# Half of one shared-expert group computed after the last routed group instead of inside the recurrence

## The chip, the cores and the metric

The kernel runs on one core of a Trainium2 chip. The metric is device time in microseconds (us) of one execution. The kernel before takes 687.25 us, the median of three runs (686.86 to 687.51).

## The reference

The input x holds 64 sequences (batch) of 64 steps with 256 features. Two layers follow each other.

1. A recurrent cell (UGRNN) scanned over the 64 steps. Each step needs the state of the step before it:

```
m = concat(x_t, h) @ weight + bias
c = tanh(m[256:]);  g = sigmoid(m[:256] + 1)
h = g * h + (1 - g) * c
```

Its outputs are added to x, which gives x1.

2. A mixture of four experts over x1 with a gate for each sequence, from means of x1 over time. Each sequence uses its best two experts. Expert 1 leaves out steps 21 to 41, expert 2 leaves out steps 0 to 20. One more expert, the shared one, serves every sequence and step. An expert is `gelu(x1 @ w1 + b1) @ w2 + b2` with 1024 hidden features. The output is x1 plus the weighted routed experts plus the shared expert.

## The kernel before, in words

All data lies with the 256 features on the partitions, as K = 2 halves of 128, and (step, sequence) along the free dimension. `acc` holds x, then x1, then the output. `x_hl` holds x1 split into a rounded high part and a low part, since every product is made of three matmuls in fp32r (high by high, low by high, high by low). All work of TensorE is recorded on one line, L722 (`mm`), so its rows are told apart by their tiles: `zy` and `hp` are PSUM.

**Expert groups.** An expert is applied to a group of up to 512 columns. A shared group is 8 steps of 64 sequences (NG = 8 groups, GT = 8 steps). A group passes through 8 chunks (NCH) of 128 hidden features. For a chunk TensorE does layer 1 (6 matmuls into `hp`, L747 to L758) and, two chunks behind, layer 2 (6 matmuls into the `zy` banks, L760 to L772). Between them ScalarE applies gelu (L322) and makes the high part (L327), and VectorE or GpSimd makes the low part (L406 in `split_lo`, or L283). Buffers for chunks are double, so chunk c waits for chunk c-2 at each stage.

**Recurrence.** Step s: 48 small bf16 matmuls of 64 columns for the state (`h_part`, L736, in three parts as the three bf16 parts of the state arrive), tanh on ScalarE (L313), then seven VectorE operations (`cell` L427 and `split_state` L417), four of them on the way to the next state. On the steps whose turn it is, TensorE also computes a quarter of the input part for the four steps to come (`x_part`, L724, 7 matmuls of 256 columns). From the second block of 8 steps on, each step carries as filler one chunk of the shared group whose steps are done (L803 to L815). So shared group 6 is worked on in the last block of 8 steps (`steps(NG - 1, ...)`, L822), and its last four steps have no `x_part`. Then shared group 7 runs alone, with the gate's small matmuls between its chunks (L826 to L847). The gate's arithmetic on VectorE is L509 to L577; between `gate_slots` and the gathering of the first routed group VectorE also writes out shared group 6 (`shared_out`, L603).

**Routed groups.** The gate puts sequences into groups of one expert: 8 sequences of 64 steps (512 columns) or 10 sequences of 44 or 43 steps (440 or 430 columns). The loops over q (the experts in the order 0, 3, 1, 2) and r (their groups) have run-time bounds `sv`. GpSimd gathers the columns of the next group (L285). After each group VectorE weighs its output (`weigh`, L611) and adds it into `acc` for each sequence (`add_slots`, L630), two or three sequences after each chunk of the next group. Sequence numbers are first loaded into registers (L592, L633, L653). `turnover` (L855) interleaves the last two layer-2 chunks of one group with the first two layer-1 chunks of the next.

**Weights.** The queue of the SyncE engine (SP) reads each expert's weights in 8 pieces of 256 KB into a ring of three stage buffers (L217 to L227). ScalarE makes a piece's high part (L333) and VectorE its low part (L414). There are two weight buffers, `w_buf[i % 2]`.

**End.** The last routed group's output is weighed and then added half by half (`add_last`, L656). The output of steps 0 to 20 is written by one DMA once no routed group can change it (L228 and L229), the rest in two DMAs of 1376 KB, one for each half of the features (L232).

Of the kernel before, what the change touches and what calls it, by code (L numbers as in the profile page):

```python
# [13 lines left out]
P = 128  # L14
# [20 lines left out]

ORDER = [E, 0, 3, 1, 2]

# [4 lines left out]
MASKED_EXPERT, MASKED_STEP = 1, HEAD  # L42
PER = [SLOTS if TOKS[e] == T else WIDE for e in ORDER[1:]]
NFULL = sum(p == SLOTS for p in PER)
# [20 lines left out]
def cond_resid_kernel(nc, x, cond, w0, b0, w_exp, small, consts, out):  # L65
    ctx = ExitStack()
    with ctx:
# [45 lines left out]
        con = sb("con", [P, C_END])  # L113
        turn = sb("turn", [P, 2])
        gs = sb("gs", [P, 96])
# [60 lines left out]
        gather_done, yw_done, add_done = sem("gather_done"), sem("yw_done"), sem("add_done")  # L176
        head_ready, out_ready = sem("head_ready"), sem("out_ready")

# [31 lines left out]
        @block.sync  # L210
        def _(sp):
            sp.dma_start(raw_w0[:, 0:K], w0[:, 0:K * 2 * D].rearrange("p (k n) -> p k n", k=K)).then_inc(s_w0, 16)
            sp.dma_start(acc[:, :, 0:GT], x[:, :, 0:GT]).then_inc(s_x0, 16)
            sp.dma_start(con[:], consts).then_inc(s_par, 16)
            sp.dma_start(par[:], small).then_inc(s_par, 16)
            sp.dma_start(acc[:, :, GT:T // 2], x[:, :, GT:T // 2]).then_inc(s_x1, 16)
            for n in range(len(ORDER) * NP):  # L217
                if n == 2:

                    sp.wait_ge(wx_split, K)  # L220
                    sp.wait_ge(wh_split, K)
# [11 lines left out]
            sp.wait_ge(s_out, 16 * (1 + K))  # L233

        @block.gpsimd
        def _(pool):
# [64 lines left out]
            for q in range(E):  # L301
                with pool.Fori(sv[q], sv[q + 1]) as r:
# [3 lines left out]
                    else:  # L306
                        gather(r, q)

        @block.scalar
        def _(act):  # L310
# [51 lines left out]
            with act.Fori(2, NG) as g:  # L362
                for i in range(GT):
                    tanh(g * GT + i, i, i // QT)
                    gelu_chunk(g - 1, i, E, 512)
            for j in range(NCH):
                if j == 1:
# [4 lines left out]
            for q in range(E):  # L372
                e = ORDER[q + 1]
                n = PER[q] * TOKS[e]
                with act.Fori(sv[q], sv[q + 1]) as r:
# [13 lines left out]
                    else:  # L389
                        for j in range(NCH):  # L390
                            gelu_chunk(r + NG, j, e, n)

        @block.vector
        def _(dve):
# [48 lines left out]

            def shared_out(g, y):

                dve.wait_ge(l2_done, (g + 1) * NCH)
                dve.wait_ge(x1_done, (g + 1) * GT)
                for k in range(K):
                    a = acc[:, k, bass.ds(g * GT, GT), :].rearrange("p t b -> p (t b)")
                    last = dve.scalar_tensor_tensor(out=a, in0=y[k], scalar=par[:, S_B2 + E * K + k:S_B2 + E * K + k + 1],  # L450
                                                    in1=a, op0=ALU.add, op1=ALU.add)
                last.then_inc(y_read, 1)
# [49 lines left out]
            with dve.Fori(2, NG) as g:  # L502
                for i in range(GT):
                    if i == 2:
                        shared_out(g - 2, yp)
                    cell(g * GT + i, i)
                    split_lo(g - 1, i, 512)

            def gate_means():  # L509
# [92 lines left out]
            gate_slots()  # L602
            shared_out(NG - 2, yp)  # L603
            dve.wait_ge(list_mm, 1)
# [36 lines left out]

            def slots_at(q, per, i):

                cuts = [0, 3, 6, 8, per] if q == E - 1 and per == WIDE else [min(2 * c, per) for c in range(NCH)]
                return list(range(cuts[i], cuts[i + 1])) if i + 1 < len(cuts) else []

# [3 lines left out]

            def batches(r, a, n):

                return nc.values_load_multi_w_load_instructions(  # L653
                    slot_b[0:1, bass.ds((r + 1) * WIDE + a, n)], engines=(mybir.EngineType.DVE,), min_val=0, max_val=B - 1)[1]

            def add_last(r, e, bs):  # L656

                n = TOKS[e]
                dve.wait_ge(y_read, r + NG + 1)
                for k in range(K):  # L660
                    for s in range(WIDE):
                        dve.wait_ge(add_done, (r + 1 + k) * WIDE + s + 1)
                        dst = tokens_of(acc[:, k:k + 1], e, bs[s])
                        src = y_w[:, k:k + 1, s * n:(s + 1) * n].rearrange("p k (a n) -> p k a n", a=RUNS[e][1])
                        dve.tensor_tensor(dst, dst, src, ALU.add).then_inc(add_done, 1)  # L665
                    dve.wait_ge(add_done, (r + 2 + k) * WIDE + 1)
                    dve.sem_inc(out_ready, 1)

# [9 lines left out]
            for q in range(E):  # L678
                e = ORDER[q + 1]
                n = PER[q] * TOKS[e]  # L680
                with dve.Fori(sv[q], sv[q + 1]) as r:

                    common = NCH - 2 if q == E - 1 else NCH
                    with dve.If(sv[q] < r):
                        for j in range(2, common):
                            split_lo(r + NG, j, n)
                            if slots_at(q, PER[q], j - 2):
                                add_slots(r, q, slots_at(q, PER[q], j - 2))
                    with dve.Else():
                        for j in range(2, common):  # L690
                            split_lo(r + NG, j, n)
                            if q == E - 1 and slots_at(q, PER[q - 1], j - 2):
                                add_prior(r, q, slots_at(q, PER[q - 1], j - 2))
                            elif q and j > 2 and slots_at(q, PER[q - 1], j - 3):
                                add_prior(r, q, slots_at(q, PER[q - 1], j - 3))
# [6 lines left out]
                    bs = []  # L702
                    for j in range(common, NCH):
                        split_lo(r + NG, j, n)
                        bs += batches(r, len(bs), WIDE - 2 if bs else 2)
                    with dve.If(r + 1 < sv[q + 1]):
# [3 lines left out]
                    with dve.Else():  # L710
                        nn = PER[q + 1] * TOKS[ORDER[q + 2]] if q < E - 1 else 0
                        if nn:
                            split_lo(r + NG + 1, 0, nn)
                        weigh(r, q)
                        if nn:
                            split_lo(r + NG + 1, 1, nn)
                        else:
                            add_last(r, e, bs)
        @block.tensor
        def _(pe):  # L720
# [53 lines left out]
            def group_src(g):  # L774
                return lambda part, k: x_hl[:, part, k, bass.ds(g * GT, GT), :]

            y0 = yp

# [12 lines left out]
            def steps(g, filler, carry, last_group=False):  # L791

                for i in range(GT):
                    s = g * GT + i
# [8 lines left out]
                    if filler:  # L803
                        f = g - 1
                        if i == 0:
                            pe.wait_ge(x1_done, g * GT)
                        layer1(f, i, w_of(0), group_src(f), 512, not carry and i < 2)
                        if i == 2 and not carry:
# [3 lines left out]
                        if i >= 2:  # L812
                            layer2(f, i - 2, w_of(0), y0, 512)
                        elif carry:
# [11 lines left out]
            for j in range(NCH):  # L826
# [27 lines left out]

            def turnover(r, i, n, w, y, r2, n2, w2):  # L855

                if n2:
                    pe.wait_ge(piece_done, i * NP + NP // 2)
                    pe.wait_ge(gather_done, r2 + 2)
                for j in range(2):  # L860
                    if n2:
                        layer1(r2 + NG, j, w2, src_of(r2, n2), n2)
                    layer2(r + NG, NCH - 2 + j, w, y, n)
# [74 lines left out]
```

## Time and profile before

| what | value |
|---|---|
| median of three runs | 687.25 us |
| profiled execution, its own time | 687.1 us |
| its span in the trace | 685.3 us |
| TensorE busy | 643.7 us (94%) |
| VectorE busy | 425.8 us (62%) |
| ScalarE busy | 289.8 us (42%) |
| GpSimd busy | 265.4 us (39%) |
| granted TensorE clock, mean | 0.988 |

Times in rows are us from the start of the span. PE is TensorE, DVE is VectorE, ACT is ScalarE, POOL is GpSimd; SPq and DVEq are the sequencers of SyncE and VectorE. In a timeline row the columns are start, duration (to the end of the last instruction merged into the row), engine, line, operation, output tile <- input tiles, count, and in brackets the engine's idle time before it with its releaser. What the chain of waits names is the work that nothing else covered.

### The profile page before, as it was taken

How to read it: one execution, taken by the hardware profiler on the slowest of the kernel's cores; microseconds unless marked ns; L12 is line 12 of the kernel's file. 1: busy time of each engine (PE TensorE's matmuls, PEld its weight loads, DVE VectorE, ACT ScalarE, POOL GpSimd, SP SyncE). 2: the span in 40 equal slices, each digit the busy share in tenths (PEclk: the TensorE clock that was granted, in tenths of full speed). 3: DMA queues.
4: the chain of work that ended last, by engine and by line, in shares of the span. 5: the costliest groups of instructions: out<-in, count | busy, mean ns of one | idle time of the engine just before them, and what ended most of it. 6: DMA issues, size and time to landing. Idle time of an engine off the chain costs nothing.

```text
span 685.3 us, 16932 instructions
## 1 busy us (share of the span) xinstructions
PE 643.7 (94%) x5752; PEld 557.7 (81%) x5752; DVE 425.8 (62%) x942; ACT 289.8 (42%) x485; POOL 265.4 (39%) x531
## 2 busy tenths in 40 slices
PE   2779999999999999999999999999999999999990
PEld 2668888888888888888768888888888999999980
DVE  5798766665656656567766655555547875555453
ACT  3224433333333333333536544544446755544540
POOL 3576646454454554534344433113321343333000
PEclk9999999999999999999999999999999999999995
DMA  6521110000000000000002100000002300000014
GB/s 247 186 64 63 48 32 2 1 0 0 0 0 0 0 0 0 0 2 2 1 0 77 46 0 0 0 0 0 0 0 78 107 18 0 0 0 0 0 64 183
DMA packets 8037, 20.97 MB, mean 31 GB/s; under 512 B 960, under 2 KB 1216, under 8 KB 7488
## 3 DMA queue, kind: packets, MB, share of 16 engines
q1 hardware_dynamic: 7568, 19.64, 8.3%
q10 hardware_dynamic: 432, 0.85, 0.3%
q8 instruction: 21, 0.34, 0.2%
q14 instruction: 16, 0.13, 0.1%
HBM read 16.30 MB, written 4.19 MB: 30 GB/s over the span
## 4 chain that ended last, share of the span: by engine, by line
PE 87%; DVE 6%; DVEq 2%; issue 2%; DMA 1%; ACT 1%; SPq 0%; POOL 0%; ACTq 0%
PE zy L722 53%; PE hp L722 33%; DMA par<-in_small 1%; DVE h_r L421 1%; DVE acc L665 1%; DVEq L633 1%; DVEq L653 1%; DVE d_t L433 1%; DVEq L592 1%; ACT uc L313 1%; DVE shared_buf L595 1%; DVE h_b L423 0%; DVE d_t L431 0%; DVE h_b L436 0%; DVE acc L639 0%
## 5 line engine op out<-in xcount | busy, mean ns | idle before, releaser
L406 DVE TENSOR_TENSOR g_lo<-g_f,g_hi 128x512 fp32r<-128x512 f32 (+2 forms) x176 | 132.9, 755 | 127.7 <-ACT g_hi L327 121.2
L322 ACT ACTIVATE g_f<-hp,par 128x512 f32<-128x512 f32 (+2 forms) x184 | 123.4, 670 | 176.5 <-PE hp L722 174.5
L722 PE MATMUL zy<-g_hi,w_buf 128*128 128x512 f32 (+2 forms) x736 | 190.7, 381 | 0.0
L722 PE MATMUL hp<-shared_buf,w_buf 128*128 (+1 forms) x720 | 173.6, 376 | 1.3 <-DVE shared_buf L595 1.3
L327 ACT ACTIVATE g_hi<-g_f 128x512 fp32r<-128x512 f32 (+2 forms) x184 | 112.9, 613 | 123.5 <-PE zy L722 123.3
L722 PEld LDWEIGHTS zy<-g_hi,w_buf 128*128 128x128 f32 x736 | 138.2, 188 | 22.7
L722 PEld LDWEIGHTS hp<-shared_buf,w_buf 128*128 128x128 f32 x720 | 135.0, 188 | 20.8 <-issue 1.9
L722 PEld LDWEIGHTS zy<-h_b,y_all 128*128 128x128 bf16 x3072 | 94.1, 98 | 27.2 <-issue 15.1
L722 PE MATMUL zy<-h_b,y_all 128*128 128x64 bf16 x3072 | 103.3, 193 | 9.4 <-DVE h_b L436 6.1
L722 PE MATMUL zy<-g_lo,w_buf 128*128 128x512 f32 (+2 forms) x368 | 110.3, 381 | 0.0
L722 PE MATMUL hp<-x_hl,w_buf 128*128 (+1 forms) x384 | 99.8, 395 | 0.3 <-POOL x_hl L254 0.3
L639 DVE TENSOR_TENSOR acc<-acc,y_all 128x128 f32 (+1 forms) x124 | 50.1, 404 | 55.2 <-issue 46.5
L251 POOL TENSOR_TENSOR x_hl<-acc,h_f 128x128 f32 (+1 forms) x64 | 31.8, 497 | 130.1 <-DVE h_f L440 130.1
L296 POOL CAST shared_buf<-x_hl x126 | 79.7, 681 | 0.0
L722 PEld LDWEIGHTS zy<-g_lo,w_buf 128*128 128x128 f32 x368 | 68.9, 188 | 11.8 <-DVE g_lo L406 0.5
L722 PEld LDWEIGHTS hp<-x_hl,w_buf 128*128 128x128 f32 x384 | 68.2, 189 | 12.6 <-POOL x_hl L254 0.8
L292 POOL TENSOR_TENSOR turn<-turn 128x1 f32<-128x1 f32 x14 | 3.4, 246 | 191.9 <-PE hp L722 187.0
L722 PE MATMUL zy<-x_hl,shared_buf 128*128 (+1 forms) x384 | 58.1, 289 | 0.0
L313 ACT ACTIVATE uc<-zy 128x256 f32<-128x256 f32 x64 | 24.6, 385 | 68.9 <-PE zy L722 68.9
L722 PEld LDWEIGHTS zy<-x_hl,shared_buf 128*128 128x128 f32 x384 | 52.3, 197 | 0.0
L241 POOL TENSOR_TENSOR x_hl<-acc,x_hl (+1 forms) x60 | 31.5, 525 | 9.6 <-POOL x_hl L239 8.7
L722 PE MATMUL zy<-shared_buf 128*128 128x256 f32 x64 | 23.5, 368 | 12.1 <-DVE x_hl L482 12.1
(109 smaller groups left out, 433.7 us busy)
## 6 DMA issues: line engine op xcount, KB each, us to landing
stage<-in_w_exp SPq DMA_DIRECT2D x40, 256.0 KB, 2.8
out_y<-acc SPq DMA_DIRECT2D x2, 1376.0 KB, 5.0
acc<-in_x SPq DMA_DIRECT2D x1, 2048.0 KB, 9.1
acc<-in_x SPq DMA_DIRECT2D x1, 1536.0 KB, 9.8
out_y<-acc SPq DMA_DIRECT2D x1, 1344.0 KB, 5.1
acc<-in_w SPq DMA_DIRECT2D x1, 512.0 KB, 4.2
acc<-in_x SPq DMA_DIRECT2D x1, 512.0 KB, 7.2
acc<-in_w ACTq DMA_DIRECT2D x1, 512.0 KB, 5.0
```

The costliest lines, as they stand in the source:

```text
L241: pool.tensor_tensor(x_hl[:, 1, :, bass.ds(s, 1), :], acc[:, :, bass.ds(s, 1), :], x_hl[:, 0, :, bass.ds(s, 1), :].bitcast(F32), ALU.subtr ...
L251: pool.tensor_tensor(hi, a, h_f[:, 1 - i % 2], ALU.add).then_inc(x1_hi, 1)
L296: last = pool.tensor_copy(dst, tokens_of(x_hl, e, bs[s]))
L313: act.activation(uc[:], zb[:, buf, :, :, i % QT, :], ACT.Tanh).then_inc(tanh_done, 1)
L322: act.activation(g_f[:, j % 2, 0:n], hp[j % 2][:, 0:n], ACT.Gelu_apprx_tanh, bias=par[:, S_B1 + e * NCH + j:S_B1 + e * NCH + j + 1]).then_ ...
L327: act.activation(g_hi[:, j % 2, 0:n], g_f[:, j % 2, 0:n], ACT.Copy).then_inc(ghi_done, 1)
L406: dve.tensor_tensor(g_lo[:, j % 2, 0:n], g_f[:, j % 2, 0:n], g_hi[:, j % 2, 0:n].bitcast(F32), ALU.subtract).then_inc(glo_done, 1)
L421: dve.tensor_tensor(h_r[:], h, h_b[:, 0], ALU.subtract).then_inc(hr_done, 1)
L433: dve.scalar_tensor_tensor(out=d_t[:], in0=uc[:, 0], scalar=1.0, in1=d_t[:], op0=ALU.add, op1=ALU.mult).then_inc(q_done, 1)
L592: bs = nc.values_load_multi_w_load_instructions(slot_b[0:1, WIDE:WIDE + SLOTS], engines=(mybir.EngineType.DVE,), min_val=0, max_val=B - 1)[1]
L639: dve.tensor_tensor(dst, dst, y_w[:, :, s * n:(s + 1) * n].rearrange("p k (a n) -> p k a n", a=RUNS[e][1]), ALU.add).then_inc(add_done, 1 ...
L722: return pe.matmul(out_, lhsT=lhsT, rhs=rhs, start=start, stop=stop, skip_group_check=True)
```

## The change

The order of experts becomes `[E, 0, 3, 1, 2, E]`. Of shared group 6 (HELD = 6) only the first four steps (HALF = 256 columns) are computed in the last block of the recurrence and at the start of group 7. The other four steps (52 to 55) are computed after the last routed group, as one more group of 256 columns. For it the shared weights are read again, as pieces 40 to 47. GpSimd makes both their high and low parts, into the buffer that the second last expert leaves. In SP's queue the DMA of output steps 0 to 20 now stands ahead of piece 45, so pieces 45 to 47 are issued behind its wait on `head_ready`. `head_ready` itself is given after all six chunks of the last expert's first group, where two sequences are added after each chunk, and no longer after four of them. The last routed group is added by `add_routed` between the chunks of the final half group, with ten sequence numbers that VectorE loads once after the loop of the first expert. Then steps 21 to 51 and 56 to 63 are written, and last the four held steps.

```diff
-ORDER = [E, 0, 3, 1, 2]
+ORDER = [E, 0, 3, 1, 2, E]
+HELD = NG - 2
+HALF = QT * B
...
@@ sync
+                if n == (len(ORDER) - 1) * NP + NP // 2 + 1:
+                    sp.wait_ge(head_ready, 1)
+                    sp.dma_start(out[:, :, 0:HEAD], acc[:, :, 0:HEAD]).then_inc(s_out, 16)
                 if n >= RING:
                     sp.wait_ge(piece_done, n - RING + 1)
...
-            sp.wait_ge(head_ready, 1)
-            sp.dma_start(out[:, :, 0:HEAD], acc[:, :, 0:HEAD]).then_inc(s_out, 16)
+            held = HELD * GT + QT
+            sp.wait_ge(routed_ready, 1)
+            sp.dma_start(out[:, :, HEAD:held], acc[:, :, HEAD:held]).then_inc(s_out, 16)
+            sp.dma_start(out[:, :, held + QT:T], acc[:, :, held + QT:T]).then_inc(s_out, 16)
             for k in range(K):
                 sp.wait_ge(out_ready, k + 1)
-                sp.dma_start(out[:, k, HEAD:T], acc[:, k, HEAD:T]).then_inc(s_out, 16)
+                sp.dma_start(out[:, k, held:held + QT], acc[:, k, held:held + QT]).then_inc(s_out, 16)
@@ gpsimd, after the gathers
+            pool.wait_ge(l2_done, (sv[E - 1] + NG) * NCH)
+            pool.tensor_tensor(turn[:, 2:3], turn[:, 0:1], turn[:, 0:1], ALU.mult)
+            for m in range(NP):
+                n, c = (E + 1) * NP + m, m * PIECE
+                w = w_of(E + 1)
+                pool.wait_ge(piece_in[n % RING], 16 * (n // RING + 1))
+                pool.tensor_copy(w[:, 0, c:c + PIECE], stage[:, n % RING]).then_inc(piece_hi, 1)
+                pool.wait_ge(piece_hi, n + 1)
+                pool.tensor_tensor(w[:, 1, c:c + PIECE], stage[:, n % RING], w[:, 0, c:c + PIECE].bitcast(F32),
+                                   ALU.subtract).then_inc(piece_done, 1)
@@ vector
-            shared_out(NG - 2, yp)
+            shared_out(HELD, yp, QT)
...
                         if q == E - 1:
-                            dve.wait_ge(add_done, (r + 1) * WIDE + 1)
+                            dve.wait_ge(add_done, r * WIDE + WIDE + 1)
                             dve.sem_inc(head_ready, 1)
...
+                if q == 0:
+                    last_bs = nc.values_load_multi_w_load_instructions(
+                        slot_b[0:1, bass.ds(sv[E] * WIDE, WIDE)], engines=(mybir.EngineType.DVE,), min_val=0, max_val=B - 1)[1]
+            final = sv[E] + NG
+            for j in range(2, NCH):
+                split_lo(final, j, HALF)
+                add_routed(slots_at(PER[E - 1], j - 2), last_bs)
+            dve.wait_ge(add_done, sv[E] * WIDE + WIDE + 1)
+            dve.sem_inc(routed_ready, 1)
+            dve.wait_ge(l2_done, final * NCH + NCH)
+            y = y_bank(sv[E])
+            for k in range(K):
+                a = acc[:, k, HELD * GT + QT:HELD * GT + 2 * QT, :].rearrange("p t b -> p (t b)")
+                dve.scalar_tensor_tensor(out=a, in0=y[k][:, 0:HALF], ..., in1=a, op0=ALU.add, op1=ALU.add).then_inc(out_ready, 1)
@@ tensor
             def steps(g, filler, carry, last_group=False):
+                src, n = (half_src(0), HALF) if last_group else (group_src(g - 1), 512)
...
-                    layer2(f - 1, NCH - 2 + j, w_of(0), y0, 512)
+                    layer2(f - 1, NCH - 2 + j, w_of(0), y0, HALF)
...
-                            turnover(r, 0, n, w, y, r + 1, 0, None)
+                            turnover(r, q + 2, n, w, y, r + 1, HALF, w_of(q + 2), half_src(1))
+            final, w = sv[E] + NG, w_of(E + 1)
+            y = y_bank(sv[E])
+            for j in range(2, NCH):
+                layer1(final, j, w, half_src(1), HALF)
+                if j == 2:
+                    pe.wait_ge(y_read, final - 1)
+                if j % 2 == 0:
+                    pe.wait_ge(piece_done, (E + 1) * NP + NP // 2 + j // 2)
+                layer2(final, j - 2, w, y, HALF)
+            pe.wait_ge(piece_done, (E + 2) * NP)
+            for j in range(NCH - 2, NCH):
+                layer2(final, j, w, y, HALF)
```

ScalarE's gelu of the last block and of the final group follows the same widths (not shown).

## Rows read from the trace of the kernel before

**Rows 1.** The page: granted clock of TensorE in tenths, 40 slices.

```profile
PEclk9999999999999999999999999999999999999995
```

**Rows 2.** The page: the chain that ended last, by engine and line.

```profile
PE zy L722 53%; PE hp L722 33%; DMA par<-in_small 1%; DVE h_r L421 1%; DVE acc L665 1%; DVEq L633 1%; DVEq L653 1%; DVE d_t L433 1%; DVEq L592 1%; ACT uc L313 1%; DVE shared_buf L595 1%; DVE h_b L423 0%; DVE d_t L431 0%; DVE h_b L436 0%; DVE acc L639 0%
```

**Rows 3.** Timeline, the recurrence's last steps and the start of shared group 7.

```profile
306.35 1.57 PE L722 MATMUL zy<-h_b,y_all 128*128 128x64 bf16 x48
...
311.42 1.57 PE L722 MATMUL zy<-h_b,y_all 128*128 128x64 bf16 x48
...
315.68 1.57 PE L722 MATMUL zy<-h_b,y_all 128*128 128x64 bf16 x48
...
325.81 0.39 ACT L313 ACTIVATE uc<-zy 128x256 f32<-128x256 f32 x1 [0.73 <-PE zy L722]
...
328.97 1.67 PE L722 MATMUL hp<-x_hl,w_buf 128*128 128x512 f32 x6 [0.34 <-POOL x_hl L254]
```

**Rows 4.** Timeline, tanh of two steps of the first block, which has no filler.

```profile
35.38 0.38 ACT L313 ACTIVATE uc<-zy 128x256 f32<-128x256 f32 x1 [3.00 <-PE zy L722]
...
39.28 0.39 ACT L313 ACTIVATE uc<-zy 128x256 f32<-128x256 f32 x1 [3.00 <-PE zy L722]
```

**Rows 5.** Timeline, from the gate's counts to the first routed group.

```profile
338.41 0.38 PE L722 MATMUL zy<-gs,d_t 64*128 64x4 f32 x2
...
344.87 1.40 DVE L450 SCALAR_TENSOR_TENSOR acc<-zy,par,acc 128x512 f32<-128x512 f32 x2
...
355.27 1.62 PE L722 MATMUL hp<-shared_buf,w_buf 128*128 128x512 f32 x6 [1.32 <-DVE shared_buf L595]
```

**Rows 6.** Chain of waits in order of time, merged: start, duration, what.

```profile
346.57 2.10 DVEq L592
...
350.67 0.18 DVEq L592
...
666.00 1.78 DVEq L653
```

**Rows 7.** Timeline of VectorE, the second expert's first group.

```profile
517.56 0.69 DVE L406 TENSOR_TENSOR g_lo<-g_f,g_hi 128x512 fp32r<-128x512 f32 x1 [0.72 <-ACT g_hi L327]
...
525.96 0.69 DVE L406 TENSOR_TENSOR g_lo<-g_f,g_hi 128x512 fp32r<-128x512 f32 x1
```

**Rows 8.** Timeline, the last routed group and the end.

```profile
650.49 1.32 PE L722 MATMUL hp<-shared_buf,w_buf 128*128 x6
...
664.37 0.61 SPq L229 DMA_DIRECT2D out_y<-acc  x1
664.41 0.94 PE L722 MATMUL zy<-g_hi,w_buf 128*128 128x430 f32 x4
...
666.54 0.65 PE L722 MATMUL zy<-g_lo,w_buf 128*128 128x430 f32 x2
670.74 1.24 DVE L618 SCALAR_TENSOR_TENSOR y_all<-zy,par,uc 128x430 f32 x2 [4.25 <-issue]
```

**Rows 9.** Groups by line and shape: GpSimd's subtraction of 512 columns and its copy of 128.

```profile
L283 POOL TENSOR_TENSOR g_lo<-g_f,g_hi 128x512 fp32r<-128x512 f32 x8 | 10.7, 1343 | 16.2 <-ACT g_hi L327 16.2
L239 POOL CAST x_hl<-acc x48 | 18.2, 379 | 0.0
```

**Rows 10.** DMAs of the page (KB each, us to landing), and the weight pieces' own landing times.

```profile
out_y<-acc SPq DMA_DIRECT2D x2, 1376.0 KB, 5.0
...
acc<-in_x SPq DMA_DIRECT2D x1, 1536.0 KB, 9.8
out_y<-acc SPq DMA_DIRECT2D x1, 1344.0 KB, 5.1
...
DMA to landing us min/median/max: 2.5/2.8/9.9
```

**Rows 11.** Windows of 1 us: busy us (instructions) of PE, PEld, DVE, ACT, POOL; granted clock, DMA share, GB/s.

```profile
668.00:669.00 1.00, 0.00 (x0) 0.00 (x0) 0.00 (x0) 0.00 (x0) 0.00 (x0) 1.00 0.96 392
669.00:670.00 1.00, 0.00 (x0) 0.00 (x0) 0.00 (x0) 0.00 (x0) 0.00 (x0) 0.69 0.01 0
```

More of the change, by code:

```diff
@@ L42 @@
 MASKED_EXPERT, MASKED_STEP = 1, HEAD
-PER = [SLOTS if TOKS[e] == T else WIDE for e in ORDER[1:]]
+PER = [SLOTS if TOKS[e] == T else WIDE for e in ORDER[1:1 + E]]
 NFULL = sum(p == SLOTS for p in PER)
@@ L361, in _ @@
                 piece_high(NP + i)
-            with act.Fori(2, NG) as g:
+            with act.Fori(2, NG - 1) as g:
                 for i in range(GT):
@@ L365, in _ @@
                     gelu_chunk(g - 1, i, E, 512)
+            for i in range(GT):
+                tanh((NG - 1) * GT + i, i, i // QT)
+                gelu_chunk(HELD, i, E, HALF)
             for j in range(NCH):
@@ L391, in _ @@
                             gelu_chunk(r + NG, j, e, n)
+            for j in range(NCH):
+                gelu_chunk(sv[E] + NG, j, E, HALF)
         @block.vector
@@ L442, in cell, with shared_out @@
                 split_state(s, h_f[:, 1 - i % 2])
-            def shared_out(g, y):
+            def shared_out(g, y, n=GT):
                 dve.wait_ge(l2_done, (g + 1) * NCH)
@@ L501, in _ @@
                 piece_low(NP + i)
-            with dve.Fori(2, NG) as g:
+            with dve.Fori(2, NG - 1) as g:
                 for i in range(GT):
@@ L507, in _ @@
                     split_lo(g - 1, i, 512)
+            for i in range(GT):
+                if i == 2:
+                    shared_out(NG - 3, yp)
+                cell((NG - 1) * GT + i, i)
+                split_lo(HELD, i, HALF)
             def gate_means():
@@ L640, in add_slots, with slots_at, add_routed @@
                                       ALU.add).then_inc(add_done, 1 if s < PER[q] - 1 else WIDE - s)
-            def slots_at(q, per, i):
-                cuts = [0, 3, 6, 8, per] if q == E - 1 and per == WIDE else [min(2 * c, per) for c in range(NCH)]
-                return list(range(cuts[i], cuts[i + 1])) if i + 1 < len(cuts) else []
+            def slots_at(per, i):
+                return [s for s in (2 * i, 2 * i + 1) if s < per]
             def add_prior(r, q, slots):
                 add_slots(r, q - 1, slots)
[L651 to L667, printed above, removed]
+            def add_routed(slots, bs):
+                e = ORDER[E]
+                for s in slots:
+                    if s == 0:
+                        dve.wait_ge(y_read, sv[E] + NG)
+                    dve.wait_ge(add_done, sv[E] * WIDE + s + 1)
+                    dst = tokens_of(acc, e, bs[s])
+                    src = y_w[:, :, s * TOKS[e]:(s + 1) * TOKS[e]].rearrange("p k (a n) -> p k a n", a=RUNS[e][1])
+                    dve.tensor_tensor(dst, dst, src, ALU.add).then_inc(add_done, 1)
             n0 = PER[0] * TOKS[ORDER[1]]
@@ L681, in _ @@
                 with dve.Fori(sv[q], sv[q + 1]) as r:
[L683 removed]
                     with dve.If(sv[q] < r):
[L685 removed]
+                        for j in range(2, NCH):
                             split_lo(r + NG, j, n)
[L687 to L688 removed]
+                            if slots_at(PER[q], j - 2):
+                                add_slots(r, q, slots_at(PER[q], j - 2))
                     with dve.Else():
[L690 removed]
+                        for j in range(2, NCH):
                             split_lo(r + NG, j, n)
[L692 to L695, printed above, removed]
+                            if q and j > 2 and slots_at(PER[q - 1], j - 3):
+                                add_prior(r, q, slots_at(PER[q - 1], j - 3))
                             if q < E - 1:
@@ L775, in group_src, with half_src @@
                 return lambda part, k: x_hl[:, part, k, bass.ds(g * GT, GT), :]
+            def half_src(a):
+                return lambda part, k: x_hl[:, part, k, HELD * GT + a * QT:HELD * GT + (a + 1) * QT, :]
             y0 = yp
@@ L806, in steps @@
                             pe.wait_ge(x1_done, g * GT)
-                        layer1(f, i, w_of(0), group_src(f), 512, not carry and i < 2)
+                        layer1(f, i, w_of(0), src, n, not carry and i < 2)
                         if i == 2 and not carry:
@@ L911 @@
     b2 = np.concatenate([rows(a, K) for a in [*g[pre + "eb2"], g[pre + "sb2"]]], axis=1)
-    routed = np.array(ORDER[1:])
+    routed = np.array(ORDER[1:1 + E])
     both = np.concatenate([routed, E + routed])
```

40 lines of the change are left out of this document (18 added, 22 removed).

## Prediction

> **What bounds the kernel now.** I read the shares of the chain of waits first: TensorE holds 86% of the span on its two PSUM tiles, and everything else is a few tenths at a time [rows 2]. Its clock stays at the full level until the last slice [rows 1]. So moving TensorE work pays only where it fills a hole or where what is hung on its end gets shorter. The timeline shows three stretches that decide about this change.
>
> The last block of the recurrence: a step takes 5.07 us with the input part (306.35 to 311.42) and 4.26 us without it (311.42 to 315.68), TensorE without a hole [rows 3]. The difference prices the seven 256-column matmuls at 0.116 us each. Taking the 1.57 us of state matmuls from 4.26 leaves 2.69 us for a filler chunk of twelve 512-column matmuls. A half chunk is 12 x 0.116 = 1.39 us or half of 2.69 = 1.35 us; I use 1.36 us as what it costs and as what it saves.
>
> The gate: after shared group 7 the first routed group waits 1.32 us for VectorE's gathering [rows 5].
>
> The end: TensorE's last matmuls end at 667.2, but VectorE begins to weigh only at 670.74, since it still loads sequence numbers, one of them for 1.78 us [rows 6, 8]. Additions and two DMAs of 1376 KB (5.0 us to landing) follow until 685.3 [rows 10]. So 18.1 us lie behind the last matmul.
>
> **The recurrence.** The cell has a latency of its own: in the first block, which has no filler, tanh follows tanh by 3.90 us (35.38 to 39.28), with TensorE waiting [rows 4]. GpSimd also splits x there, which it no longer does in the last block, so 3.90 is the upper end; the lower end is what TensorE needs, 5.07 - 1.36 = 3.71. I take 3.75. Seven step-to-step intervals lie ahead of the last tanh at 325.81 [rows 3]:
> - the first two still carry layer 2 of group 5 at full width, so each saves only layer 1's half, 0.68: 1.36;
> - two more with input part go from 5.07 to 3.75: 2.64;
> - the three without it would need 2.90 of TensorE, but the latency holds them at 3.75, from 4.26: 1.53;
> - `shared_out` of group 5 (1.40 at this width, as in [rows 5]) stands ahead of the third cell on VectorE and was hidden in 5.07; now it delays the cell by some 0.3.
>
> Together 5.2 us, where TensorE's own work falls by 7 x 1.36. The first matmul of group 7 (328.97) waits for GpSimd's last addition, 3.16 us behind that tanh [rows 3]; this is unchanged, so 5.2 stays. Bounds: 4.3 (latency 3.90) and 5.6 (3.71 and no delay).
>
> **The gate.** The counts' matmul at 338.41 comes after the two layer-2 chunks of group 6, which are halved: 1.36. From there on VectorE sets the pace. `shared_out` at 344.87 goes from 1.40 to some 0.95, 0.45 more. The gathering and the first routed group at 355.27 thus come 5.2 + 1.36 + 0.45 = **7.0 us earlier** [rows 5]. The remaining 3.9 us of the 10.9 us (8 x 1.36) of removed TensorE work become holes.
>
> **Ten register loads after the loop of the first expert.** A load costs 0.28 us in a row of them (0.18 and the issue), but the first of a long batch took 1.78 and 2.10 [rows 6], of a short one less: 3.3 to 4.9 us. They stand ahead of the `split_lo` at 517.56, which had waited 0.72 for ScalarE; later in this group VectorE is saturated, as 525.96 has no idle time ahead of it [rows 7], so lateness is kept. Its low parts are ready 2 to 3.5 us before TensorE wants them. I take 0.7, bounds 0 and 3.
>
> **The reloaded weights.** The last expert has one group here, whose chunks j = 2 to 7 run from 650.49 to 664.41 [rows 8]. GpSimd may start when the group before has ended, about 650.8. A piece is a subtraction of 512 columns, 1.34, and a copy of 512. The trace has the copy of 128 only, 0.38 [rows 9]: from 0.6 (a small slope) to 1.5 (four of them); I take 1.0, and 2.45 for the piece. Pieces 40 to 43 are done at 660.8 and turnover begins at 664.4, so no wait there; piece 44 follows at 663.3.
>
> Piece 45 is different. SP reaches it only after `head_ready`, which now comes after all six chunks: the last low part at 665.9, then two additions with their loads, 667.45. SP issues the 1344 KB output DMA, and behind it the pieces. That DMA takes 5.1 to landing [rows 10]: 672.6. The queue serves in order: the first weight pieces at the start, issued 0.6 behind the 1536 KB that took 9.8, took 9.9 themselves, against 2.8 in the median [rows 10]. A piece of 256 KB is 0.65 at 392 GB/s [rows 11], so piece 45 lands at 673.25 and GpSimd finishes 45, 46, 47 at 675.7, 678.2, 680.6.
>
> TensorE: turnover with two added half layer-1 chunks ends at 668.1 (before 667.2 with its small waits). Three layer-1 and two layer-2 half chunks follow, until 671.5. Then it stands 4.2 us for piece 45. In the trace before, the clock fell 2.2 us after the last matmul (0.69 of the window 669 to 670 [rows 11]), so I expect the fall to half. What lies between there and the last low part is 42 matmuls, 4.9 us at full and 9.7 us at half level. Nothing in the trace shows when it rises again; I take the middle, 7.3, so 683.0. With high and low part of the last chunk and semaphores, 1.1, the routed additions' release is at 684.1 (bounds 681.7 and 686.5).
>
> The Trainium skill, "TensorE: Matmul & The Clock Gate", "Part 1: The HAM clock gate", says that an idle array is throttled and that activity releases it; this trace shows the fall only. By that rule the rest wouldn't all run at half level, which speaks for the middle rather than for 686.5. The sum doesn't rest on it.
>
> **The end.** Behind that release: output of 39 steps (2.56 MB) and, in the same queue, the four held steps (0.26 MB), 2.82 MB at some 410 GB/s, 6.8 us; 1.2 from issue to first byte (664.37 to about 665.6) and 1.3 from the last byte to the end of the span: 9.3 us. The held steps' two additions (0.45 each) lie beside it. End 684.1 + 9.3 = 693.4 against 685.3: **8.1 us later** for an unchanged start. ScalarE's extra 16 operations lie in TensorE's shadow, GpSimd was idle after 631.
>
> **The sum.** -7.0 + 0.7 + 8.1 = +1.8 on the profiled execution (span 685.3, its own time 687.1). That time is 0.15 under the median, so I add to the median: **689.0 us**.
>
> **The rivals.**
> - Clock kept. TensorE stands for 4.2 us but resumes at full level, or work piles up so that it is not the limit: release 681.7, end +5.7, sum -0.6: 686.6. For it: the whole run shows no second fall. Against: 2.2 us sufficed.
> - Pieces not behind the output (faster). The reads of 45 to 47 come through beside the output DMA and land 2.8 after issue, at 671.0. Piece 45 is done at 673.4, the stand is 1.9, under the 2.2 that the clock bore, release 679.5, end +3.5: sum -2.8, 684.4. Together with a copy on GpSimd of 0.6 it reaches 683. It decides from a landing before 671.3. Against: the 9.9 us landing at the start. A cell latency of 3.6 or less would add 1 us to it.
> - Clock low to the end, loads dear: 686.5 for the release, 2.5 for the loads: sum -7.0 + 2.5 + 10.5 = +6.0, 693.3. For it: VectorE saturated in [rows 7], and GpSimd's operations get longer beside VectorE's.
> - The hole is closed by TensorE alone: recurrence bound by TensorE to its end, all 10.9 us saved, with the rest as forecast: 685.1. Against: [rows 4].
>
> **The numbers.** Forecast 0.44, clock kept 0.20, pieces beside 0.15, low to the end 0.13, recurrence all saved 0.08. Faster or slower by 0.2% is 1.4 us here, about what a measurement tells from no change. The forecast's own spread is 687 to 691, so a third of it falls within 0.2%; clock kept falls within it mostly. Faster 0.27, same 0.28, slower 0.45. Range 684.0 to 692.8.
>
> **What would show it.** Tanh to tanh in the last block: 3.75 us, group 7's first matmul at 323.8, first routed group at 348.3. TensorE without idle time near 510 to 520 says that the loads cost nothing. Piece 45's first copy on GpSimd 5 to 6 us behind the issue of the 1344 KB output; TensorE idle some 4 us before the final group's third layer-2 chunk, and half clock behind it. Last matmul some 15 us ahead of the end. The prediction is wrong if TensorE never waits for a weight piece, or if the recurrence saves over 6 us.

## The result and the profile after

The changed kernel takes 689.55 us (median of 8 runs, 688.85 to 691.56) against 687.08 us for the kernel before, measured beside it (8 runs). The ratio is 1.0041, 95% interval 1.0031 to 1.0051: 2.8 us slower, between 2.1 and 3.5.

Counted by stages, each from a row of before to the same row of after (profiled executions, us):

| stage | before | after | difference | forecast |
|---|---|---|---|---|
| start to the last block of steps | 291.13 | 290.43 | -0.7 | 0 |
| to shared group 7 | 37.84 | 32.70 | -5.14 | -5.2 |
| to the first routed group | 26.30 | 25.25 | -1.05 | -1.8 |
| to the last expert's group | 295.22 | 296.41 | +1.19 | +0.7 |
| to the end of the span | 34.81 | 42.91 | +8.10 | +8.1 |
| span | 685.3 | 687.7 | +2.4 | +1.8 |

The first line is no effect: nothing is changed there, and this point lay between 290.0 and 291.6 in the profiles of all kernels here. The four lines below it, which the change touches, add up to +3.1 us.

The recurrence after, in the timeline; tanh of the last block's third and fourth step, three more, and group 7, to be held beside [rows 3]:

```profile
300.91 0.39 ACT L333 ACTIVATE uc<-zy 128x256 f32<-128x256 f32 x1 [0.94 <-PE zy L751]
304.98 0.38 ACT L333 ACTIVATE uc<-zy 128x256 f32<-128x256 f32 x1 [1.25 <-PE zy L751]
...
312.50 0.38 ACT L333 ACTIVATE uc<-zy 128x256 f32<-128x256 f32 x1 [1.77 <-PE zy L751]
316.25 0.38 ACT L333 ACTIVATE uc<-zy 128x256 f32<-128x256 f32 x1 [1.76 <-PE zy L751]
320.00 0.38 ACT L333 ACTIVATE uc<-zy 128x256 f32<-128x256 f32 x1 [1.77 <-PE zy L751]
...
323.13 1.67 PE L751 MATMUL hp<-x_hl,w_buf 128*128 128x512 f32 x6 [1.66 <-POOL x_hl L263]
```

From the fifth step on, tanh follows tanh by 3.75 us where it was 4.26. The interval 300.91 to 304.98 is 4.07, since the output of group 5 stands ahead of the cell on VectorE: the 0.3 of the forecast. TensorE now stands 1.66 us ahead of group 7 where it stood 0.34.

The gate and the first routed group, beside [rows 5]:

```profile
331.29 0.38 PE L751 MATMUL zy<-gs,d_t 64*128 64x4 f32 x2
...
338.16 0.86 DVE L475 SCALAR_TENSOR_TENSOR acc<-zy,par,acc 128x256 f32<-128x256 f32 x2
...
344.16 4.11 DVE L626 CAST shared_buf<-x_hl 128x256 fp32r x8 [4.88 <-issue]
...
348.38 1.61 PE L751 MATMUL hp<-shared_buf,w_buf 128*128 128x512 f32 x6 [1.18 <-DVE shared_buf L626]
```

This stretch is not the same in every profile. In ten profiles of kernels with this part of the change it is 25.2 to 25.5 us in seven and 24.4 us in three (the filled stand, the prior additions and the high parts on ScalarE, below). In the first of the three the eight copies that gather the first routed group take 3.11 us in place of 4.11:

```profile
344.85 3.11 DVE L626 CAST shared_buf<-x_hl 128x256 fp32r x8 [4.87 <-issue]
```

Why, no run shows. So the gain is 1.05 to 1.9 us, and the table has its lower end.

The loop end of the first expert, beside [rows 7]:

```profile
509.23 0.69 DVE L431 TENSOR_TENSOR g_lo<-g_f,g_hi 128x512 fp32r<-128x512 f32 x1 [0.23 <-DVE y_all L649]
515.03 0.69 DVE L431 TENSOR_TENSOR g_lo<-g_f,g_hi 128x512 fp32r<-128x512 f32 x1 [5.11 <-issue]
```

The low part that waited 0.72 us for ScalarE now comes after 5.11 us of register loads, and TensorE waits 0.9 us for it.

The last expert's group starts here, to be held beside 650.49 in [rows 8]:

```profile
644.79 1.33 PE L751 MATMUL hp<-shared_buf,w_buf 128*128 x6
```

The end: the chain of waits in order of time (start, duration, what), merged.

```profile
661.98 0.61 SPq L230
662.64 6.35 DMA stage<-in_w_exp
669.04 0.62 POOL w_buf L324
669.73 1.27 POOL w_buf L326
671.05 1.60 PE zy L751 x6
672.65 1.28 PE hp L751 x6
673.93 1.05 PE zy L751 x6
674.98 0.71 PE hp L751 x6
```

The chain reads as the forecast's sentence: the output DMA is issued at 661.98, piece 45 behind it needs 6.35 us to land (2.7 in the median), GpSimd splits it, TensorE goes on, its first groups of six matmuls in 1.60 and 1.28 us where a later one takes 0.71. The same place in the timeline and the later rows:

```profile
671.05 1.18 PE L751 MATMUL zy<-g_hi,w_buf 128*128 128x256 f32 x4 [4.82 <-POOL w_buf L326]
...
678.54 0.59 SPq L237 DMA_DIRECT2D out_y<-acc  x1
679.00 0.40 PE L751 MATMUL zy<-g_lo,w_buf 128*128 128x256 f32 x2
...
680.23 2.25 SPq L241 DMA_DIRECT2D out_y<-acc  x2
```

The windows of 1 us, columns as in [rows 11]:

```profile
670.00:671.00 1.00, 0.00 (x0) 0.00 (x0) 0.00 (x0) 0.00 (x0) 1.00 (x2) 1.00 0.00 0
671.00:672.00 1.00, 0.95 (x4) 0.95 (x5) 0.00 (x0) 0.00 (x0) 0.92 (x2) 0.57 0.00 0
673.00:674.00 1.00, 1.00 (x7) 1.00 (x6) 0.80 (x2) 0.20 (x2) 0.92 (x2) 0.50 0.00 0
674.00:675.00 1.00, 1.00 (x8) 1.00 (x8) 1.00 (x1) 0.44 (x1) 0.86 (x1) 0.73 0.06 16
```

From the release at 678.54 to the end of the span are 9.2 us; in [rows 8] 18.1 us lay behind the last matmul, now 8.3. In what follows, "the stand" is TensorE's idle time ahead of 671.05, and "the release" is the issue of the output at 678.54, which waits for VectorE's last routed addition.

### The profile page after: what moved, and what is told of

The parts are those of the page before. It is cut to its first block, busy times and chain, and to the rows that moved or that the text cites. A ratio compares the mean times of both kernels' runs of the same rounds, so it can differ in the third digit from the quotient of the medians.

```text
span 687.7 us, 17160 instructions
## 1 busy us (share of the span) xinstructions
PE 647.2 (94%) x5848; PEld 565.2 (82%) x5848; DVE 426.8 (62%) x942; ACT 293.1 (43%) x501; POOL 285.7 (42%) x548
## 4 chain that ended last, share of the span: by engine, by line
PE 85%; DVE 7%; DVEq 2%; DMA 2%; issue 2%; ACT 1%; POOL 0%; SPq 0%; ACTq 0%
PE zy L751 52%; PE hp L751 32%; DVE h_r L446 1%; DMA par<-in_small 1%; DMA stage<-in_w_exp 1%; DVE d_t L458 1%; ACT uc L333 1%; DVE h_b L448 1%; DVEq L732 1%; DVE d_t L456 1%; DVEq L623 1%; DVE h_b L461 1%; DVE shared_buf L626 1%; DVEq L664 0%; DVE g_lo L431 0%
## 5 line engine op out<-in xcount | busy, mean ns | idle before, releaser
L431 DVE TENSOR_TENSOR g_lo<-g_f,g_hi 128x512 fp32r<-128x512 f32 (+3 forms) x184 | 134.1, 729 | 133.8 <-ACT g_hi L347 124.0
L342 ACT ACTIVATE g_f<-hp,par 128x512 f32<-128x512 f32 (+3 forms) x192 | 125.4, 653 | 176.7 <-PE hp L751 172.6
L751 PE MATMUL zy<-g_hi,w_buf 128*128 128x512 f32 (+3 forms) x768 | 193.3, 374 | 4.8 <-POOL w_buf L326 4.8
L347 ACT ACTIVATE g_hi<-g_f 128x512 fp32r<-128x512 f32 (+3 forms) x192 | 114.5, 596 | 126.0 <-PE zy L751 125.3
L751 PEld LDWEIGHTS zy<-g_hi,w_buf 128*128 128x128 f32 x768 | 141.6, 189 | 26.4 <-POOL w_buf L326 5.0
L751 PE MATMUL zy<-g_lo,w_buf 128*128 128x512 f32 (+3 forms) x384 | 111.9, 373 | 0.9 <-DVE g_lo L431 0.9
L751 PE MATMUL hp<-x_hl,w_buf 128*128 (+2 forms) x432 | 102.1, 372 | 1.7 <-POOL x_hl L263 1.7
L305 POOL CAST shared_buf<-x_hl x126 | 83.2, 709 | 0.0
L751 PEld LDWEIGHTS hp<-x_hl,w_buf 128*128 128x128 f32 x432 | 73.0, 191 | 12.2 <-POOL x_hl L263 1.9
L751 PEld LDWEIGHTS zy<-g_lo,w_buf 128*128 128x128 f32 x384 | 71.3, 189 | 11.9 <-DVE g_lo L431 1.3
```

Of the source, the lines that this page charges most:

```text
L305: last = pool.tensor_copy(dst, tokens_of(x_hl, e, bs[s]))
L342: act.activation(g_f[:, j % 2, 0:n], hp[j % 2][:, 0:n], ACT.Gelu_apprx_tanh, bias=par[:, S_B1 + e * NCH + j:S_B1 + e * NCH + j + 1]).then_ ...
L347: act.activation(g_hi[:, j % 2, 0:n], g_f[:, j % 2, 0:n], ACT.Copy).then_inc(ghi_done, 1)
L431: dve.tensor_tensor(g_lo[:, j % 2, 0:n], g_f[:, j % 2, 0:n], g_hi[:, j % 2, 0:n].bitcast(F32), ALU.subtract).then_inc(glo_done, 1)
L751: return pe.matmul(out_, lhsT=lhsT, rhs=rhs, start=start, stop=stop, skip_group_check=True)
```

## The experiments

Each ratio is to the kernel before, measured beside it; the changed kernel's is 1.0041 (1.0031 to 1.0051). 0.1% is 0.69 us.

**The order in SP's queue.** The output DMA of steps 0 to 20 goes behind the loop over the pieces:

```diff
-                if n == (len(ORDER) - 1) * NP + NP // 2 + 1:
-                    sp.wait_ge(head_ready, 1)
-                    sp.dma_start(out[:, :, 0:HEAD], acc[:, :, 0:HEAD]).then_inc(s_out, 16)
...
+            sp.wait_ge(head_ready, 1)
+            sp.dma_start(out[:, :, 0:HEAD], acc[:, :, 0:HEAD]).then_inc(s_out, 16)
             held = HELD * GT + QT
```

> The changed kernel with one thing undone: the output DMA of steps 0 to 20 stands behind all weight pieces in SP's queue, not ahead of piece 45. Theory (piece 45 is late because it waits for head_ready and then behind 1344 KB, and the stand also costs half the clock): TensorE's stand of 4.8 us goes, the clock stays full, so the 42 matmuls up to the release take 4.9 us in place of 6.9; together 6.8 us, from 689.55 to about 682.8 (ratio to before 0.9937). Rival (GpSimd's splitting of the pieces is too slow by itself): GpSimd would still be late, 1 to 3 us saved, 687 to 688. Rival (VectorE's additions hold the release): 2 to 4 us saved, 686 to 687.

685.04 us, ratio 0.9971 (0.9959 to 0.9984): 4.8 us under the changed kernel and faster than the kernel before. From the last expert's group (645.97) to the release (674.92) are 28.95 us, where they were 33.75. The stand is gone, and with it the half clock (mean granted clock 0.997). Two of the expected 6.8 us are missing. 0.8 of them were never there: half clock cost 1.2 us and not 2.0 (the filled stand below). The rest shows in the timeline, where VectorE's additions now meet GpSimd's pieces 46 and 47:

```profile
660.24 2.15 DVE L669 TENSOR_TENSOR acc<-acc,y_all 128x88 f32 x2 [1.10 <-issue]
660.60 0.94 PE L750 MATMUL zy<-g_hi,w_buf 128*128 128x430 f32 x4
...
660.92 1.29 POOL L325 TENSOR_TENSOR w_buf<-stage,w_buf 128x512 fp32r<-128x512 f32 x1
...
663.17 1.88 DVE L669 TENSOR_TENSOR acc<-acc,y_all 128x88 f32 x2
...
666.06 0.50 PE L750 MATMUL zy<-g_lo,w_buf 128*128 128x256 f32 x2 [0.91 <-DVE g_lo L430]
```

Two additions of 128x88 take 2.15 and 1.88 us beside GpSimd, where the changed kernel has 0.83 and 0.82 at this point with GpSimd idle, and TensorE waits 0.91 for the low part behind them, 1.4 us with two shorter waits beside it (0.25 and 0.22).

**Wait or queueing.** Pieces 45 to 47 still wait for `head_ready`, but are issued ahead of the output DMA:

```diff
                 if n == (len(ORDER) - 1) * NP + NP // 2 + 1:
                     sp.wait_ge(head_ready, 1)
-                    sp.dma_start(out[:, :, 0:HEAD], acc[:, :, 0:HEAD]).then_inc(s_out, 16)
...
+            sp.dma_start(out[:, :, 0:HEAD], acc[:, :, 0:HEAD]).then_inc(s_out, 16)
```

> The changed kernel, but pieces 45 to 47 keep their wait on head_ready and the output DMA of steps 0 to 20 goes behind them: the wait stays, the queueing behind 1344 KB goes. Theory (the queueing is what hurts): piece 45 is issued at 662.0 and lands 2.7 later at 664.7, split by 666.6, where TensorE asks at 666.2; stand 0.4 and full clock: 6.4 us saved, about 683.2. Rival (the wait on head_ready is most of the lateness): stand of 3 us or more and half clock stay, under 2.5 us saved, 687 or more.

685.08 us, ratio 0.9976 (0.9967 to 0.9985), the same as the experiment before within both intervals, and not the 683.2 expected. GpSimd begins piece 45 at 665.58:

```profile
665.58 0.61 POOL L325 CAST w_buf<-stage 128x512 fp32r<-128x512 f32 x1 [8.63 <-DMA stage<-in_w_exp]
```

The piece took 3.35 us to land where 2.7 was expected. TensorE stands 1.4 us, the clock stays at 1.00, and from the last expert's group (644.98) to the release (674.19) are 29.21 us. So the 1344 KB ahead of the pieces cost 3.4 of the 4.8 us of stand, and the half clock with them; what is left of the wait is 1.4 us of stand. That this kernel still ends level with the other has its reason in the rows: at turnover GpSimd is idle and VectorE's additions of two sequences take 0.83 us. They take 1.95 and 2.10 us beside GpSimd only later, where TensorE waits for none of them.

**The clock alone.** Forty matmuls whose result nobody reads fill the stand:

```diff
+                if j == 4:
+                    for _ in range(40):
+                        mm(gp[:, 0:HALF], w[:, 0, 0:P], half_src(1)(0, 0), True, True)
                 if j % 2 == 0:
                     pe.wait_ge(piece_done, (E + 1) * NP + NP // 2 + j // 2)
```

> The changed kernel, with 40 matmuls of 256 columns more, whose result nobody reads, where TensorE stands before the third layer-2 chunk of the final half group. They take 4.6 us of a stand of 4.8. Theory (the stand costs a further 2.0 us by half clock behind it): granted clock stays 1.00 and the 42 matmuls up to the release take 4.9 us in place of 6.9: 687.5. Rival (behind the stand the pieces 46 and 47 set the pace, done at 672.9 and 674.9, or the DMA end hides it): under 0.5 us saved, 689.1 or more, or slower if the additional matmuls outlast the stand.

688.97 us, ratio 1.0032 (1.0021 to 1.0043); against 1.0041 the intervals overlap, so the times alone do not settle it. The traces do:

```profile
665.94 4.96 PE L751 MATMUL zy<-x_hl,w_buf 128*128 128x256 f32 x40
671.05 0.74 PE L751 MATMUL zy<-g_hi,w_buf 128*128 128x256 f32 x4
...
677.37 0.59 SPq L237 DMA_DIRECT2D out_y<-acc  x1
```

TensorE resumes at 671.05 in both kernels, but the release comes 6.32 us later here and 7.49 in the changed kernel. Half clock costs 1.2 us, not the 2.0 expected: it lasted only 3.4 us of the remaining work.

**The register loads.** First spread over three loop ends in the changed kernel:

```diff
-                if q == 0:
-                    last_bs = nc.values_load_multi_w_load_instructions(
-                        slot_b[0:1, bass.ds(sv[E] * WIDE, WIDE)], ...)[1]
+                if q < E - 1:
+                    a, z = (0, 4, 7, WIDE)[q:q + 2]
+                    last_bs += nc.values_load_multi_w_load_instructions(
+                        slot_b[0:1, bass.ds(sv[E] * WIDE + a, z - a)], ...)[1]
```

> The changed kernel, with VectorE's ten register loads after the loop of the first expert split into 4, 3 and 3 after the loops of the first three experts. Theory (one batch of ten makes a low part 1.2 us late for TensorE, three short ones stay within the slack): no idle time of TensorE near 515, 1.2 us saved, 688.35. Rival (the first load after a loop is dear by itself, 2.3 us, wherever it stands): each batch still takes over 3 us and TensorE waits at one or more loop ends, 0 to 0.5 us saved or a loss.

690.36 us, ratio 1.0056 (1.0042 to 1.0070). This did not help. The theory held for the middle: from the first routed group to the last expert's group are 295.18 us, as in the kernel before (295.22), where the changed kernel has 296.41. But the third batch holds VectorE in the last expert's group, and `head_ready` comes after VectorE:

```profile
662.09 0.61 SPq L230 DMA_DIRECT2D out_y<-acc  x1
...
670.15 0.61 POOL L324 CAST w_buf<-stage 128x512 fp32r<-128x512 f32 x1 [15.22 <-DMA stage<-in_w_exp]
```

The DMA is issued at 662.09, no earlier than 661.98, so the 1.2 us gained are lost again: a gain in the middle is worth nothing here if VectorE is then held ahead of `head_ready`. The loss beyond that is another matter. Piece 45 lands 7.35 us after its issue in place of 6.35, and the stand is 6.0 us. Why it landed 1.0 us later, no run shows; it is not shown that the batches are the cause.

Then the loads alone, added to the kernel before:

```diff
+                if q == 0:
+                    nc.values_load_multi_w_load_instructions(
+                        slot_b[0:1, bass.ds(sv[E] * WIDE, WIDE)], ...)
```

> The kernel before with the ten register loads of the change added after the loop of the first expert, and nobody uses them. Theory (they hold VectorE for 5 us at the one place where it is then saturated, and TensorE waits 0.9 us and 0.3 us for low parts): 1.2 us slower, 688.2 (ratio 1.0017). Rival (slack hides them; the 1.2 us between the first routed group and the last has another cause, such as gathers or pieces): 687.0.

688.40 us, ratio 1.0023 (1.0014 to 1.0032): 1.6 us slower, 1.0 to 2.2. The trace has the hole on VectorE at the same place, and TensorE waits 1.3 us for the low part:

```profile
514.96 0.69 DVE L406 TENSOR_TENSOR g_lo<-g_f,g_hi 128x512 fp32r<-128x512 f32 x1 [0.22 <-DVE y_all L618]
521.11 0.69 DVE L406 TENSOR_TENSOR g_lo<-g_f,g_hi 128x512 fp32r<-128x512 f32 x1 [5.46 <-issue]
```

**The first half of the change alone.** The kernel before with half of group 6 as filler. The other half, the shared expert's part of steps 52 to 55, is left out, so its output lacks that part:

```diff
+                src, n = (half_src(0), HALF) if last_group else (group_src(g - 1), 512)
...
-                    layer2(f - 1, NCH - 2 + j, w_of(0), y0, 512)
+                    layer2(f - 1, NCH - 2 + j, w_of(0), y0, HALF)
...
-            shared_out(NG - 2, yp)
+            shared_out(HELD, yp, QT)
```

> The kernel before, with only the first half of the change: the last recurrence block and the start of shared group 7 carry half of shared group 6, and the other half (the shared expert's part of steps 52 to 55) is left out altogether. Nothing else is changed. Theory: the two traces, each counted from the start of the last block of steps, give 5.1 us up to group 7 and 6.2 us up to the first routed group, and behind that nothing differs: 687.1 - 6.2 = 680.9 (ratio 0.991). Rival (TensorE time is what counts everywhere): all 10.9 us of removed TensorE work, 676.2. Rival (given back at the end): 684 or more.

679.58 us, ratio 0.9891 (0.9876 to 0.9906): 7.5 us less, 6.5 to 8.5. In its trace group 7 begins 32.70 us after the last block's start, as in the changed kernel, and the first routed group 58.15 us (64.14 before): 6.0 us. The times give more than the trace; 0.5 us of it is the start (290.65 against 291.13), which is no effect. In any case it is far from the 10.9 us of TensorE work that are gone: the recurrence's latency and the gate's work on VectorE keep the rest.

**Towards a better version.** With pieces first, VectorE's prior additions at chunks 2 to 5:

```diff
+                            cuts = [0, 3, 6, 8, WIDE]
+                            if q == E - 1 and j < 6:
+                                add_prior(r, q, list(range(cuts[j - 2], cuts[j - 1])))
```

> The kernel with the weight pieces ahead of the output DMA (e1_pieces_first), and in the last expert's first group VectorE adds the group before as the kernel before did: three, three, two and two sequences after chunks 2 to 5, not two after each of the chunks 3 to 7. Theory (without the stand, GpSimd splits pieces 45 to 47 just while VectorE makes its last additions and both get longer: two additions took 2.15 us in place of 0.82, and TensorE waits 0.9 and 0.2 us for low parts): the additions are over before, 1.1 to 2 us less than e1_pieces_first, about 683.5. Rival (it was the low parts and the weighing themselves that GpSimd lengthens, not the additions): no difference, 685.0; chunk 2 to 5 may then even be late, up to 1 us more.

684.92 us, ratio 0.9970 (0.9958 to 0.9982): no difference from 685.04. The output DMA is issued at 661.48, and additions of 1.80 us for two now stand at 654.85: GpSimd works through the whole group, so the additions meet it wherever they are put. TensorE's waits for low parts stay at 2.1 us in all (2.0 with pieces first), of which 0.9 is the wait behind the register loads.

The release of the last routed output after chunk 5:

```diff
-                add_routed(slots_at(PER[E - 1], j - 2), last_bs)
-            dve.wait_ge(add_done, sv[E] * WIDE + WIDE + 1)
-            dve.sem_inc(routed_ready, 1)
+                cuts = [0, 3, 6, 8, WIDE]
+                if j < 6:
+                    add_routed(list(range(cuts[j - 2], cuts[j - 1])), last_bs)
+                if j == 5:
+                    dve.wait_ge(add_done, sv[E] * WIDE + WIDE + 1)
+                    dve.sem_inc(routed_ready, 1)
```

> e1_pieces_first with one thing more: the last routed group is added with three, three, two and two sequences at chunks 2 to 5 of the final half group, and its output released right then, not after chunk 7. Theory (9.2 us of output follow the release, so each us of it counts in full): in e7_all the release came 1.6 us ahead of the last TensorE work where it came 0.1 us ahead in e1_pieces_first, so 1.3 to 1.7 us less than e1_pieces_first: 683.5. Rival (the held steps' own output, behind the last TensorE work, sets the end): under 0.5 us less, 684.6 or more.

683.01 us, ratio 0.9948 (0.9934 to 0.9961), 1.6 us under pieces first. The two intervals just meet, but the traces agree with the times: the release comes at 672.19, 27.25 us after the last expert's group (28.95 without), and the end 9.1 us behind it. All three together with the loads in three batches:

> The version to which the experiments point: pieces ahead of the output DMA, additions in the last expert's group at chunks 2 to 5, the ten register loads in three batches, and the last routed group added with three, three, two and two sequences at chunks 2 to 5 of the final half group and released right then. Theory: 1.1 us from the loads (they cost through head_ready only where pieces wait behind it), 1.5 to 2.5 us from the earlier release, since 9.2 us of output follow it: 4 us below e1_pieces_first at best, 680.5 to 682. Rival (VectorE's three additions and a low part, 1.65 us, exceed TensorE's 1.4 us a chunk and delay low parts as much as they advance the release): 683 to 684.

683.42 us, ratio 0.9947 (0.9934 to 0.9961): no better than the early release alone, and not the 680.5 to 682 expected. The three batches do give 1.2 us in the middle (295.17), but from the last expert's group to the release are 28.86 us in place of 27.25, and TensorE's waits for low parts are 2.5 us. That this is the third batch on VectorE, as above, is likely and not shown by itself.

Last, ScalarE makes the high parts, as it does for the other experts (the branch that splits weights in an expert's first group now holds for the last expert too, and GpSimd's copy goes):

```diff
-                    if q < E - 1:
-                        with act.If(sv[q] < r):
...
+                    with act.If(sv[q] < r):
...
-                pool.wait_ge(piece_in[n % RING], 16 * (n // RING + 1))
-                pool.tensor_copy(w[:, 0, c:c + PIECE], stage[:, n % RING]).then_inc(piece_hi, 1)
```

> e9_early_release, and ScalarE makes the high parts of the reloaded weights as it does for the other experts, so that GpSimd only subtracts. Theory (GpSimd's work at turnover lengthens VectorE's additions, 2.15 us for two in place of 0.82, and makes TensorE wait 1.1 us for low parts): GpSimd is through before turnover, TensorE's waits there go, 1 to 1.5 us less than e9_early_release: 682.3. Rival (GpSimd now goes at ScalarE's pace, one piece a chunk, still works at turnover, and ScalarE's additional 0.62 us a piece delays gelu): no gain or a loss of up to 1 us.

681.25 us, ratio 0.9929 (0.9916 to 0.9943), the lowest median here: 4.9 us under the kernel before. Against the kernel it was made from the intervals overlap, and TensorE's waits fell only from 2.0 to 1.6 us, since GpSimd goes at ScalarE's pace, as the rival said; its last subtractions end at about 663 in both:

```profile
657.76 1.58 POOL L323 TENSOR_TENSOR w_buf<-stage,w_buf 128x512 fp32r<-128x512 f32 x1 [0.73 <-ACT w_buf L350]
660.08 2.93 POOL L323 TENSOR_TENSOR w_buf<-stage,w_buf 128x512 fp32r<-128x512 f32 x2 [0.74 <-ACT w_buf L350]
```

So whether this step gained at all, and whether by the mechanism named, is open.

## Why the prediction was right

Forecast 689.0 us, measured 689.55 us. The mechanism was right in all four stages, but the hit is closer than the sum deserves. As a difference the forecast was +1.8 us. The ratio gives +2.8 (2.1 to 3.5), and the four stages of the table add up to +3.1: 0.75 too little was taken for the gate and 0.5 for the loads. The span's +2.4 lies nearer only because the start, where nothing is changed, happened to be 0.7 us shorter.

- **Recurrence, 5.2: right to 0.1.** The interval of 3.75 us, the two steps that stay bound by TensorE and the 0.3 of the earlier output are all in the rows. The rival in which all 10.9 us are saved is refuted by the half of the change run alone.
- **Gate, 1.8 expected, 1.05 measured.** The counts' matmul came 1.28 us nearer to group 7's start, as 1.36 said. The 0.45 of the halved output (0.86 in place of 1.40) were lost again: from that matmul to the first routed group are 17.09 us where they were 16.86. VectorE's output is shorter by 0.54, but L583 (L552 before) takes 0.49 in place of 0.19 us, L586 (L555 before) 1.03 in place of 0.93, and from the first register load to the gathering are 4.84 us in place of 4.48. Part of the miss may be chance, since this stretch is 0.85 us shorter in three of the ten profiles.
- **Loads, 0.7 expected, 1.2 in the trace and 1.6 (1.0 to 2.2) alone.** Without the batch of ten (the three batches) the 1.2 us are gone from the trace. The batch took 5.11 us of VectorE, just over the upper price of 4.9, and 0.7 had been chosen for a price in the middle. The mechanism was right, the size was low.
- **Stand, 4.2 expected, 4.8 measured**, from the same cause: 1344 KB ahead in the queue. The order of pieces shows it (4.8 us in the ratio), and the separation of wait and queueing puts 3.4 of the 4.8 us on the queueing. From the issue of the output to the landing of piece 45 are 7.0 us, where 5.8 were expected (5.1, and 0.65 at 392 GB/s); between 666 and 668 the windows show 237 and 228 GB/s.
- **GpSimd.** Its copy of 512 takes 0.61, the low end of the range, not 1.0, and its subtraction 1.26 to 1.70. A piece is 1.9 to 2.4 us. Only the splitting of piece 45 hung on this, since the pieces waited for the DMA: 2.0 us from its landing to TensorE's resumption, where 2.45 were expected.
- **Clock.** It fell and rose. That the rest would run at half level for a middle share was right in kind: 1.2 us by the filled stand, against 2.4 in my middle. A longer stand (by 0.6), reached 0.4 later, and a smaller loss (by 1.2) made up for each other; GpSimd's cheaper piece is part of the 4.8 already.
- **The end, 8.1 expected, 8.10 measured.** 9.2 us from release to end against 9.3. The match to the hundredth is luck: the last group's rows differ by up to 1.2 us from mine with both signs.
- **The signs.** Piece 45's first copy came 7.1 us behind the issue of the output, not 5 to 6, for the reason given at the stand. "Last matmul some 15 us ahead of the end" contradicts the forecast's own sum, which has 9.3 us behind the release; measured are 8.3. The 683 in the rival with pieces beside the output does not follow from its terms either: a copy of 0.6 takes 0.4 from 684.4, which is 684.0.

## What to carry to other kernels

Work moved out of a loop with a latency of its own frees only what lay over that latency: count the interval's lower bound before counting the engine time removed. A transfer that something waits for should not stand behind a large output in the same queue, even when both are free to go: here that cost 3.4 us of stand and 1.2 us of half clock. What follows the last release counts in full, so bring the release forward rather than the last matmul.

## What was not expected of the hardware

- The granted clock did not fall at a fixed distance from the last matmul: 2.2 us behind it in [rows 11], but in the changed kernel it was still 1.00 in the window 670 to 671, 4.8 us behind, and fell as work resumed. It was back at full level 3.5 us after the resumption (0.73 in the window 674 to 675). With the loads in three batches the stand is of the same kind, and there it fell 2.1 us behind the last matmul (666.14), within the stand, and was back 2.9 us after the resumption at 672.16:

```profile
668.00:669.00 1.00, 0.00 (x0) 0.00 (x0) 0.00 (x0) 0.00 (x0) 0.00 (x0) 0.63 0.89 302
```

- Ten register loads on VectorE take 5.1 to 5.5 us at a loop end, of which the first 2.3.
- GpSimd's copy of 128x512 takes 0.61 us, less than half of its subtraction (1.26 to 1.70), and two VectorE additions of 128x88 take 0.83 us with GpSimd idle and up to 2.15 beside GpSimd. The subtraction itself is no longer where the additions are: 1.29 us beside the 2.15.
